# Autocorrelation attention: a second fold of the weights' lags, with two product sums and one fold done by accumulating DMAs

## The reference

```
corr = ifft(fft(q, axis=2) * conj(fft(k, axis=2)), axis=2).real
w, idx = top_k(corr.transpose(0, 1, 3, 2), 12);  w = softmax(w)
for i in range(12):
    g = minimum(idx[:, :, None, :, i] + pos, L - 1)
    out = out + w[:, :, None, :, i] * take_along_axis(v, g, axis=2)
```

## Time and profile before

| | |
|---|---|
| timed runs | 2239.7, 2241.87, 2241.94 us (median 2241.87) |
| profiled execution | span 2240.4 us; the page gives no other time of it |
| busy, share of the span | PE 97%, PE's weight loads 65%, DVE 76%, POOL 70%, ACT 55% |
| attention's loop | to about 1365 us; the expert half follows |
| granted TensorE clock | 0.9 or more in each of the 40 slices |

### The profile page before, as it was taken

One profiled execution on the slowest core, in us unless ns is written; L12 is line 12 of the kernel. 1 busy time (PEld: TensorE's weight loads), 2 busy tenths in 40 slices (PEclk: granted clock), 3 DMA queues, 4 the chain that ended last, 5 costly groups with the idle time before them and its releaser, 6 DMA issues.

```text
span 2240.4 us, 30428 instructions
## 1 busy us (share of the span) xinstructions
PE 2170.8 (97%) x9664; PEld 1460.5 (65%) x9664; DVE 1712.2 (76%) x4081; ACT 1222.0 (55%) x2486; POOL 1570.1 (70%) x1023
## 2 busy tenths in 40 slices
PE   4899999999999999999999998899999999999999
PEld 2466565565565565565565564687888888787887
DVE  7999999999999999999999999744544444454443
ACT  4576676676676676676655535544434334443431
POOL 6899999999999999999999987433333333333420
PEclk9999999999999999999999999999999999999999
DMA  8132332332332332332321245544444444444431
GB/s 288 65 120 99 111 110 99 116 106 99 118 104 99 118 104 99 118 103 99 103 82 61 91 164 176 186 157 164 151 162 166 167 160 161 157 159 161 164 116 57
DMA packets 110420, 287.84 MB, mean 128 GB/s; under 512 B 7136, under 2 KB 7264, under 8 KB 109152
## 3 DMA queue, kind: packets, MB, share of 16 engines
q1 hardware_dynamic: 110304, 286.45, 37.1%
HBM read 219.32 MB, written 67.11 MB: 128 GB/s over the span
## 4 chain that ended last, share of the span: by engine, by line
PE 77%; DVE 11%; POOL 5%; issue 4%; ACT 2%; DMA 1%; SPq 0%; DVEq 0%; POOLq 0%; ACTq 0%
PE pair L691 7%; PE out L528 5%; PE out L530 5%; PE out L529 5%; PE z L528 5%; PE z L530 5%; PE z L529 5%; PE evac L602 4%; PE evac L603 4%; PE pair L528 4%; PE evac L578 4%; PE pair L530 4%; PE pair L529 4%; PE lag L642 4%; PE pair L591 4%
## 5 line engine op out<-in xcount | busy, mean ns | idle before, releaser
L1549 POOL TENSOR_TENSOR rows<-rows,cin 128x1024 f32<-128x1024 f32 x48 | 117.9, 2456 | 355.8 <-DMA rows<-out_dram 292.8
L691 PE MATMUL pair<-r_f,back 128*128 128x512 f32 x768 | 335.4, 593 | 0.0
L1495 POOL TENSOR_TENSOR r_f<-prod 128x1024 f32<-128x1024 f32 x128 | 306.0, 2402 | 24.0 <-DVE prod L931 22.1
L691 PEld LDWEIGHTS pair<-r_f,back 128*128 128x128 f32 x768 | 143.3, 190 | 167.8 <-issue 167.8
L528 PE MATMUL pair<-w_hi,wts_hi 128*128 128x512 f32 x512 | 206.5, 403 | 4.9 <-DVE w_lo L1049 2.9
L1244 ACT ACTIVATE xt_full<-tp 128x512 f32<-128x512 f32 x128 | 74.8, 584 | 245.4 <-PE tp L547 242.0
L528 PE MATMUL out<-b_hi,zt_hi 128*128 128x512 f32 x512 | 205.8, 402 | 1.5 <-ACT zt_hi L1433 1.5
L528 PE MATMUL z<-a_hi,xt 128*128 128x512 f32 x512 | 203.0, 397 | 1.9 <-DVE xt L888 1.9
L530 PE MATMUL pair<-w_hi,wts_lo 128*128 128x512 f32 x512 | 200.5, 392 | 0.0
L529 PE MATMUL pair<-w_lo,wts_hi 128*128 128x512 f32 x512 | 200.4, 391 | 0.0
L529 PE MATMUL z<-a_lo,xt 128*128 128x512 f32 x512 | 200.1, 391 | 0.0
(11 more groups left out here) (193 smaller groups left out, 5619.2 us busy)
## 6 DMA issues: line engine op xcount, KB each, us to landing
out_dram<-att_sb SPq DMA_DIRECT2D x32, 1024.0 KB, 4.3
rows<-out_dram SPq DMA_DIRECT2D x64, 512.0 KB, 3.6
cin<-out_dram SPq DMA_DIRECT2D x64, 512.0 KB, 4.0
xin<-in_x_dram SPq DMA_DIRECT2D x64, 512.0 KB, 3.7
out_dram<-rows SPq DMA_DIRECT2D x64, 512.0 KB, 2.6
vf<-in_ctx_dram SPq DMA_DIRECT2D x31, 1024.0 KB, 5.2
xf<-in_x_dram SPq DMA_DIRECT2D x30, 1024.0 KB, 5.1
stat_in<-in_x_dram SPq DMA_DIRECT2D x28, 1024.0 KB, 5.1
```

The costliest lines, as they stand in the source:

```text
L691: return nc.tensor.matmul(pair_ps[:, bank, :], back[:, 3 * bank + n, :], r_f[:, row, :], start=n == 0, stop=n == 2)
L1495: nc.gpsimd.tensor_tensor(dst, prod[:, slot, 0:2, :], prod[:, slot, 2:4, :], ALU.add).then_inc(add_done, 1)
L1549: nc.gpsimd.tensor_tensor(half, first, second, op).then_inc(c_added, 1)
```

## The change

- The lags of the weights are folded a second time. `fold_w` now takes two tiles at once and waits for both: two operations of 508 elements as before, three of 2, then two more of 508. A spectrum of the weights needs one or two blocks of lags in each part where it needed two: 12 products, 36 matmuls, where there were 16 and 48.
- Products: DVE writes the first factor's pair straight into `p_f` or `r_f` and the second into `prod`, which now has four slots. For x (2 sets) and the odd-frequency weights (2 sets) POOL adds them in place by two operations of 512 elements. The other two sets of the weights (`cyc`) are added by two accumulating DMAs from POOL's queue (`send_products`, 512 KB each), on which PE's last `out_row`s wait. Each of these two sets takes DVE one operation of 1024 elements and two of 512.
- ctx's first fold is an accumulating DMA of 1024 KB (`sum_ctx`, on POOL's queue, in front of the second `fold_w`) over `ctx_sum`, loaded twice, and `ctx_add`, whose negative ACT makes. Two POOL operations of ctx's fold go. `end_fold_x` moves to the end of POOL's step.
- DVE's sums of the lags, ACT's copies for them, the negated maximum, the memset and the reciprocal take two tiles at once: half the operations, twice the elements. ACT's four `minus` and two `middle_copy` a step go; `put_constant` (L1386 before) stands between row sums and squares.

```diff
+        W_TERMS = (((0, SUM),), ((1, REST_OFF),)), (((2, OFF),), ((3, REST_SUM),)), \
+            (((4, REST_SUM), (5, REST_OFF)), ((6, SUM), (7, OFF))), (((8, REST_SUM), (9, REST_OFF)), ((10, SUM), (11, OFF)))
...
+                if i >= 1 and i + 2 < GROUPS:
+                    sp.wait_ge(ctx_summed, 16 * i)
+                    load_far(k, r, 2)
+                    sp.wait_ge(v_ready, i + 2)
+                    load_near(k, r, 2)
...
-                        for h in range(2):
-                            t = 4 * blk + 2 * part + h
+                        for t, l in terms:
                             last = split_mm(pair_ps[:, 2 * (n % 2) + part, :], wts_hi[:, t, :], wts_lo[:, t, :],
-                                            w_hi[:, first + h, :], w_lo[:, first + h, :], h == 0, h == 1)
+                                            w_hi[:, l, :], w_lo[:, l, :], t == terms[0][0], t == terms[-1][0])
...
-                    pe.wait_ge(add_done, prod_w(i, 2) + 1)
-                    pe.wait_ge(dc_put, i)
+                    pe.wait_ge(cyc_summed, 16 * i)
...
-                    pe.wait_ge(add_done, prod_w(i, 3) + 1)
+                    pe.wait_ge(odd_summed, 16 * i)
...
+                def products_x(n):
+                    cos_v, turned_v = v_cyc[cur][:, 2 * n:2 * n + 2, :], v_cyc[cur][:, 2 * n:2 * n + 2, :][:, ::-1, :]
+                    nc.vector.tensor_tensor(p_f[:, 2 * n:2 * n + 2, :], of_pair(n, 0), cos_v, ALU.mult)
+                    nc.vector.tensor_tensor(prod[:, n, :, :], of_pair(n, 1), turned_v, ALU.mult).then_inc(prod_ready, 1)
...
+                    dve.wait_ge(cos_copied, pair_at(i, t))
+                    nc.vector.tensor_tensor(cos_ps, cos_in, sin_ps, ALU.add).then_inc(lag_folded, 1)
+                    dve.wait_ge(lag_folded, corr_at(i, t, 0))
+                    nc.vector.tensor_tensor(sin_ps, cos_in, sin_ps, ALU.subtract).then_inc(lag_folded, 1)
...
+                    dve.wait_ge(low_copied, pair_at(i, t))
+                    nc.vector.tensor_tensor(total, high, low, ALU.add).then_inc(corr_summed, 1)
+                    dve.wait_ge(corr_summed, corr_at(i, t, 0))
+                    nc.vector.tensor_tensor(low, high, low, ALU.subtract).then_inc(corr_summed, 1)
...
+                    act.wait_ge(lag_ready, CT * i + t + 2)
+                    nc.scalar.activation(e[:, both, 0:2 * P], lag_ps[:, :, 0:2 * P], ACT.Copy).then_inc(cos_copied, 1)
...
                     row_sums(i + 2)
+                    put_constant()
...
+                if i + 2 < GROUPS:
+                    act.wait_ge(far_loaded, 16 * (i + 1))
+                    nc.scalar.activation(ctx_add[:, 2:4, :], ctx_add[:, 0:2, :], ACT.Copy, scale=-1.0).then_inc(far_negated, 1)
...
+            def sum_ctx(g):
...
+                pool.wait_ge(near_loaded, 32 * (g - 1))
+                pool.wait_ge(far_negated, g - 1)
+                nc.gpsimd.dma_start(ctx_sum[:], ctx_add[:], accum_op=ALU.add).then_inc(ctx_summed, 16)
...
             def add_products(idx, slot, dst):
                 pool.wait_ge(prod_ready, idx + 1)
-                nc.gpsimd.tensor_tensor(dst, prod[:, slot, 0:2, :], prod[:, slot, 2:4, :], ALU.add).then_inc(add_done, 1)
+                nc.gpsimd.tensor_tensor(dst[:, 0, :], dst[:, 0, :], prod[:, slot, 0, :], ALU.add)
+                nc.gpsimd.tensor_tensor(dst[:, 1, :], dst[:, 1, :], prod[:, slot, 1, :], ALU.subtract).then_inc(add_done, 1)
...
+            def send_products(i, n, signal):
+                blk = W_BLOCKS[n]
+                pool.wait_ge(prod_ready, prod_w(i, n) + 1)
+                nc.gpsimd.dma_start(r_f[:, 2 * blk:2 * blk + 2, :], prod[:, n, :, :], accum_op=ALU.add).then_inc(signal, 16)
...
+                pool.wait_ge(weighted, CT * g + t + 2)
...
+                nc.gpsimd.tensor_tensor(sums, up, down, ALU.add).then_inc(folded, 1)
+                nc.gpsimd.tensor_tensor(rests, up, down, ALU.subtract).then_inc(folded, 1)
...
+                nc.gpsimd.tensor_tensor(offs, near, far, ALU.subtract).then_inc(folded, 1)
+                nc.gpsimd.tensor_tensor(near, near, far, ALU.add).then_inc(folded, 1)
```

More of the change, by code:

```diff
@@ L919, in body, with of_pair @@
                 cur, before = (r + 1) % 2, r % 2
[L921 to L931 removed]
+                def of_pair(pair, part, wide=2):
+                    bank = pair_ps[:, 2 * pair + part, :]
+                    return bank.unsqueeze(1).broadcast_to((P, 2, CH)) if wide == 2 else bank
@@ L1615, in body @@
                     add_half(1, 0, 1, 1)
-                if f and not is_step(i, 0):
-                    end_fold_v(i + 1)
+                if f and b:
+                    end_fold_x(i + 1)
                 if is_step(i, 0):
```

326 lines of the change are left out of this document (163 added, 163 removed).

## The result

The kernel after takes **2566.39 us** (four timed runs, 2565.34 to 2566.53), the kernel before 2241.66 (four runs with it, 2239.7 to 2241.94): a ratio of 1.145, 95% interval 1.1434 to 1.1466. The forecast was 2378 us, its range 2315 to 2432. The direction was right, the size was not: +325 us instead of +136. The profiled execution has a span of 2563.5 us.

What follows compares the result with a forecast made beforehand. The prediction took a loop of waits over POOL's second fold, through DVE and ACT, as the bound: 41.5 us a step becoming 45.95. The 4.45 over 29 steps gave +129, entry and exit +7: 2378 us, range 2315 to 2432.

Steps and rivals of the forecast that it cites:

- Top-k and choice: one negation, one memset and one reciprocal fewer, 6.65 instead of 6.86.: DVE's stretch after the weights' products in the loop: three operations fewer, 6.65 us instead of 6.86.
- The loop over POOL's second fold, its 45.95: Waits from one second fold of POOL (tiles 2 and 3) to the next, through DVE and ACT: 45.95 us against 41.5.
- Both with the same `variance`: Steps with `variance`, one in four, about 1.1 us longer, were assumed to add the same before and after.
- The second fold as the main price: POOL's fold of the weights' lags: 5.4 us instead of 3.05, +2.4, twice in the loop.
- DVE's order would close at 44.7: DVE's own sequence of work would close at 44.7 us a step, with POOL ending last by about a microsecond.
- PE's 12 matmuls worth nothing: PE's 12 fewer matmuls save 2.8 us of work a step, but were called worth next to nothing by themselves.
- PE has some waits under its 41.47: PE, shown busy 41.47 of 41.50 us in the kernel before, was said to include waits, since matmuls overlap in the records.
- Accumulating DMAs: The two DMAs of products: nearest rows 3.6 and 5.1 us, up to double; cost nothing, cover up to 9 us.
- the cover of 17 us for the other DMA: `sum_ctx` may take 17 us, since POOL has nothing else to do until S + 17.9, S being its second fold's start.
- 1 (issue or landing dear): Rival: issue or landing of accumulating DMAs is dear; at 3 us an issue, some 2470 us; chance 0.1.
- 2 (clock): Rival: PE's granted clock falls to 0.8, PE bounds the step, +5.5 to 6 us a step, about 2415 us; chance 0.05.
- 3 (wide operations cheap): Rival: POOL's operations of 508 elements cost little more than 254; step some 40.7 us, about 2210 us; chance 0.1.

Runs made afterwards that it cites:

- experiment 1: Kernel after, with the negated maximum as two operations of one element again instead of one paired operation; 2391.07 us, ratio 1.0672 to before.
- experiment 2: Kernel before, with only the negated maximum of two tiles made one 128x2 operation; 2283.91 us, ratio 1.0191.
- experiment 5: Kernel after, with the paired negation made from two inputs instead of one; 2566.44 us, ratio 1.1455.
- experiment 6: Kernel after, paired negation kept, with POOL waiting on a semaphore between the two operations of `end_fold_x`; 2500.70 us, ratio 1.1159.
- experiment 7: Kernel after, paired negation kept; the first operation of `end_fold_x` signals a semaphore but nobody waits for it; 2567.15 us, ratio 1.1455.
- experiment 8: Kernel after, paired negation kept, with the two accumulating DMAs of product sums replaced by POOL additions; 2437.72 us, ratio 1.0872.
- experiment 10: Experiment 1's kernel without the two wide operations of the weights' second fold, so its weights are not the attention's; 2323.22 us, ratio 1.0365.
- experiment 4: Experiment 1's kernel with `begin_fold_x` moved behind ctx's first fold operation; 2367.51 us, ratio 1.0567.
- experiment 11: Experiment 4's kernel with the choice of tiles 2 and 3 ahead of the output's last sum on DVE; 2351.35 us, ratio 1.0490.
- experiment 12: Experiment 11's kernel with DVE's sums of the lags and ACT's copies for them by single tile again; 2344.27 us, ratio 1.0459.
- experiment 3: Kernel before with 36 instead of 48 matmuls for the weights' spectra, leaving out half the lags of two sets; 2232.06 us, ratio 0.9964.
- experiment 13: Kernel before with only the choice of tiles 2 and 3 moved ahead of the output's last sum on DVE; 2319.78 us, ratio 1.0341.
- 15: Kernel before with only the memset and the reciprocal of two tiles made one operation each; 2246.57 us, ratio 1.0021.

## Why the prediction was wrong in size, step by step

- **The failed step: "Top-k and choice: one negation, one memset and one reciprocal fewer, 6.65 instead of 6.86."** I priced the pair as one operation fewer by its count. It is an operation of another kind, with a wait of its own: 5.79 us for tiles 0 and 1, 0.98 for tiles 2 and 3, where two single ones take 0.22. What the runs showed in its place: it waits until GpSimd's operation under way has ended, and behind a DMA issue for the ones that follow. With it split the time is 2391, 13 us (0.5%) from the 2378 forecast; the pair is 175 of the 325 us (experiment 1). I had even drawn on the Trainium skill's page on the shared port, but for GpSimd's descriptors only, and didn't ask it of DVE's own operations. No row that I had read shows the operation, so by my own method it should have had a bound from the rows of POOL, that is the rest of POOL's run. The trace of before did hold the warning, in the expert half, DVE and then POOL:

```profile
1427.53 2.17 DVE L908 TENSOR_TENSOR norm_x<-norm_x 128x1 f32<-128x1 f32 x1
```

```profile
1425.42 4.26 POOL L1552 TENSOR_TENSOR rows<-xin,rows 128x1024 f32<-128x1024 f32 x1
```

A product of two single numbers from SBUF, 0.16 us in 30 of its 32 places, takes 2.17 here and ends at 1429.70 with POOL's operation (1429.68); two more such places (0.30 us at 1368.41, 2.31 at 1399.02, L914) end with one too.
- Where the lock comes from. Shown: the pair ends with a POOL operation in all 64 places (after, experiments 2, 5, 6, 7, 8), the single negations do not wait, and the pair waits with one SBUF input and with two (experiment 5). The Trainium skill, page "SBUF — State Buffer", section "Who interferes with whom", has DVE and GpSimd share one pair of ports: whichever issues first holds it for the whole instruction, and this holds for two-port modes of DVE and, against a GpSimd operation that reads SBUF, also for its operations with two SBUF inputs; by the page "VectorE: DVE Perf Modes", section "What auto-detection actually checks", an operation with a single source takes the two-port mode if source and destination are in SBUF and their outer dimensions are even. By these rules the negation of an even pair waits for GpSimd and that of a single number does not, and the trace agrees: 965 ns at least for 128x2, 155 at most for 128x1, and the product above, with two inputs, waits at 128x1. That the wait spans several operations behind a DMA issue is shown by experiments 6 and 8 alone. Not every operation of 128x2 waits; DVE and POOL of experiment 1:

```profile
625.82 0.15 DVE L1043 RECIPROCAL inv_sum<-exp_sum 128x2 f32<-128x2 f32 x1
```

```profile
625.53 2.36 POOL L1512 TENSOR_TENSOR half_fold<-xf 128x1024 f32<-128x1024 f32 x1
```

The reciprocal takes at most 0.17 us in all 64 places, 61 of them under an operation of POOL. That the mode is the reason was not tried by itself.
- The loop over POOL's second fold, its 45.95: **right**, 45.88 in experiment 1, each station within 0.4 us. Fold 5.33 (5.4), `begin_fold_x` 4.62 (4.65), sums' idle 2.93 (2 to 3); the issue is 0.6 (1.0), which makes up for a first fold that comes 0.4 late. "Both with the same `variance`" was too low: over the plain step the mean of 29 is 0.6 us more in experiment 1 (46.48, from 116.22 to 1464.28) and 0.3 before (41.78), about 9 of the 13 us.
- The second fold as the main price: **right in kind**, 68 us by experiment 10 of the 150 that experiment 1 still loses. The rest is then no longer additive: experiments 4, 11 and 12 take 24, 16 and 7 us away and each runs into another wait, on PE's late spectra, on its clock or on ACT.
- "DVE's order would close at 44.7": 45.3 (experiment 4). What it lacked is PE behind DVE: the sums free PSUM banks, PE fills them, DVE waits again.
- PE's 12 matmuls worth nothing: **right**, 8 us (experiment 3). But "PE has some waits under its 41.47" was half the truth: with the output's last sum later, PE lost time at once (experiment 13). My reading of the kernel before had DVE's order last by 1.8 us; taking matmuls from PE brings 8 us (experiment 3), taking operations from DVE costs 5 (15) and choosing earlier 78 (13). That suggests loops that close nearly together; for POOL's it was not tried.
- Accumulating DMAs: landing 6.4 and 11.3 us, where I had "up to double" 3.6 and 5.1; the second is above it. PE waits 2.29 us for the products in the transform back (L728, in the step shown; 78.6 us in all), which I had named as a sign of being wrong, though at a landing above 9. DVE comes to that result at 639.93, 9 us after PE has made it, so the wait is outside the loop, and the cover of 17 us for the other DMA held.
- The rivals: 1 (issue or landing dear) named the right neighbours, GpSimd, DVE and the DMA queue, and the wrong direction: GpSimd was not held up by DVE, DVE was by GpSimd. An issue costs 0.6 us. 2 (clock): 1.00 in the step shown, 0.97 over the span and below 1.00 in 24 of the 29 steps of after, the sign that I had named. It did not set the time there: 51.6 us are found at 1.00 and at 0.97 alike, as 45.88 in experiment 1. Where PE's lateness reaches the loop it costs 1.7 us a step (experiment 13). 3 (wide operations cheap) is refuted by 508 elements at 1.22 us from start to start; its own sum was off too, 41.5 - 40.7 is 0.8 and not 1.1 a step.

**Still open:** why a semaphore wait of POOL's own ends the lock-out behind an issue; how the 82 us that are left of experiment 1's loss without the second fold (experiment 10) divide among the waits. No run was made for either.

## What to carry to other kernels

Pairing two small DVE operations does not halve the cost when the paired form has to wait for GpSimd: the negation of two numbers in SBUF did, that of one did not. Ask of each small operation on SBUF whether it waits for GpSimd, and keep one that does out of the stretches where GpSimd works. One element of width is no safeguard for two SBUF inputs (2.17 us in the kernel before). If a small operation is shown with a duration near that of another engine's, compare their ends before anything else. In a step where several loops close within a microsecond, a rearrangement must be followed through the PSUM banks it frees, not only through the engine it relieves.

## What the runs showed of the hardware that I had not expected

- DVE's TENSOR_SCALAR and SCALAR_TENSOR_TENSOR of 128x2 in SBUF wait for GpSimd's operation under way (0.20 to 1.61 us in experiment 8), and where a DMA issue stands in GpSimd's queue, for what follows it too: 5.79 us in the step shown and 6.88 at most. RECIPROCAL of 128x2 does not (0.17 at most), and TENSOR_TENSOR of 128x1 with two SBUF inputs does (0.30, 2.17 and 2.31 us where GpSimd was at work in the kernel before, 0.16 elsewhere; one of them a SCALAR_TENSOR_TENSOR). A wait on a semaphore between GpSimd's operations cut it to 3.50 and made the kernel 66 us faster.
- Behind a DMA issue, GpSimd's operations of 1024 elements are shown as 2.97 us instead of 2.36, though their starts are still 2.31 apart.
- In the kernel after, an accumulating DMA from SBUF to SBUF of 512 KB lands after 6.4 us, one of 1024 KB after 11.3 (medians).
- Half the granted clock for 3.4 us, where PE is what the loop waits for, makes a step 1.7 us longer (experiment 13); where it is not, nothing (experiment 1).
